# Negated score maxima: from four-row scratch and small transfers to rows written in place

## The reference

```python
xn = layernorm(layernorm(x), gamma, beta)
q = (xn @ w_q).reshape(B, 256, 16, 64);  k, v = split(context @ w_kv)      # 16 heads of 64
attn = softmax(einsum('bqhd,bkhd->bhqk', q * 64 ** -0.5, k))
x = x + tanh(g_xattn) * (einsum('bhqk,bkhd->bqhd', attn, v) @ w_out + b_out) * tanh(gate)
# then a mixture of 8 experts: top-1 routing, 160 slots each, relu(t @ w1[e]) @ w2[e]
x = x + tanh(g_ffn) * experts(layernorm(x))
```

## Time and profile before

| | |
|---|---|
| device time, median of 3 runs | 587.85 us (586.03 to 588.67) |
| the profiled execution's own time | 586.77 us |
| its span in the trace | 585.0 us |
| PE busy | 506.5 us, 87% |
| DVE busy | 436.3 us, 75% |
| ACT busy | 360.5 us, 62% |
| POOL busy | 338.2 us, 58% |
| DMA traffic | 91.22 MB, 156 GB/s on average |
| mean granted TensorE clock | 0.961 of full speed |

### The profile page before, as it was taken

How to read it: one execution, slowest core, us unless ns; L and a number is a source line. 1 busy time by engine, 2 the same in 40 slices (tenths; PEclk the granted TensorE clock), 3 DMA queues, 4 the chain that set the end, 5 groups by cost and what they waited for, 6 DMA issues and landing times.

```text
span 585.0 us, 16296 instructions
## 1 busy us (share of the span) xinstructions
PE 506.5 (87%) x5644; PEld 447.7 (77%) x5644; DVE 436.3 (75%) x814; ACT 360.5 (62%) x671; POOL 338.2 (58%) x207
## 2 busy tenths in 40 slices
PE   4657988799989998999899998999899989985294
PEld 3446877698879887888789887988788879775194
DVE  4577977579886889878987988698869897876112
ACT  3445767467765776667675776577667765762041
POOL 4553568637584657646664666466647565665115
PEclk9877999899999999999999999999999999999588
DMA  7886778847785778757775777677757766750201
GB/s 197 192 220 176 188 190 193 212 99 176 167 203 135 171 162 195 164 129 177 167 177 129 174 166 182 140 176 166 172 130 174 166 154 154 167 149 15 91 4 41
DMA packets 48686, 91.22 MB, mean 156 GB/s; under 512 B 6515, under 2 KB 21539, under 8 KB 48656
## 3 DMA queue, kind: packets, MB, share of 16 engines
q1 hardware_dynamic: 47280, 87.53, 64.9%
q0 software_dynamic: 1376, 3.30, 1.6%
HBM read 10.83 MB, written 5.14 MB: 27 GB/s over the span
## 4 chain that ended last, share of the span: by engine, by line
PE 41%; SPq 27%; DMA 11%; issue 8%; DVE 6%; ACT 4%; POOL 1%; DVEq 0%; POOLq 0%; ACTq 0%
SPq L416 10%; DMA ST<-MROW 8%; SPq L418 7%; PE psS L1107 6%; SPq L428 5%; PE psS L1108 5%; PE psX L1187 4%; PE psM L1083 4%; PE psO L1128 3%; PE psO L1130 2%; PE psO L1129 2%; DVE MX L805 2%; ACT P L662 2%; SPq L433 2%; PE psKQ L1021 2%
## 5 line engine op out<-in xcount | busy, mean ns | idle before, releaser
L558 POOL TENSOR_TENSOR PARTS<-P,PARTS 128x1024 f16<-128x1024 f32 x128 | 274.6, 2146 | 182.9 <-ACT PARTS L706 114.3
L662 ACT ACTIVATE P<-psS 128x512 f32<-128x512 f32 x256 | 146.3, 599 | 62.6 <-PE psS L1108 57.3
L805 DVE TENSOR_REDUCE MX<-psM 128x2 f32<-128x1024 f32 x128 | 155.8, 1217 | 15.9 <-PE psM L1083 15.1
L1107 PE MATMUL psS<-ST 128*128 128x256 f32 x512 | 144.9, 310 | 25.3 <-DMA ST<-MROW 20.4
L1107 PEld LDWEIGHTS psS<-ST 128*128 128x128 f32 x512 | 97.7, 191 | 44.0 <-issue 27.1
L1108 PE MATMUL psS<-ST 128*128 128x256 f32 x512 | 131.0, 283 | 0.0
L1128 PE MATMUL psO<-VH,PARTS 128*128 128x65 f16 x1024 | 108.1, 196 | 2.2 <-POOL PARTS L558 1.6
L1129 PE MATMUL psO<-VL,PARTS 128*128 128x64 f16 x1024 | 106.9, 193 | 0.0
L1130 PE MATMUL psO<-VH,PARTS 128*128 128x65 f16 x1024 | 106.6, 194 | 0.0
L622 ACT ACTIVATE HL<-psKQ 128x768 fp32r<-128x768 f32 x62 | 50.4, 812 | 79.7 <-PE psKQ L1023 76.4
L1108 PEld LDWEIGHTS psS<-ST 128*128 128x128 f32 x512 | 98.4, 192 | 1.0
(11 more groups left out here) (168 smaller groups left out, 818.8 us busy)
## 6 DMA issues: line engine op xcount, KB each, us to landing
ST<-HL SPq DMA_DIRECT2D x128, 384.0 KB, 5.4
ST<-HL SPq DMA_DIRECT2D x128, 192.0 KB, 4.9
ctx_raw<-in_ctx_dram SPq DMA_DIRECT2D x8, 256.0 KB, 4.7
ST<-MROW SPq DMA_DIRECT2D x128, 1.0 KB
w1s<-in_L_ffn_w_dram SPq DMA_DIRECT2D x8, 256.0 KB, 4.7
w2s<-in_L_ffn_w_dram SPq DMA_DIRECT2D x8, 256.0 KB, 3.2
experts_table<-O POOLq DMA_DIRECT2D x2, 645.0 KB, 8.0
PARTS<-experts_table SPq DMA_DIRECT2D x2, 516.0 KB, 4.2
```

The costliest lines, as they stand in the source:

```text
L558: pool.tensor_tensor(PLO[:, par, h, :], P32[:, h, :], PHI[:, par, h, :], ALU.subtract).then_inc(plo_done, 1)
L662: act.activation(P32[:, h, 512 * (c % 2):512 * (c % 2) + 512], psS[c % 2][:], ACT.Exp, scale=SCALE).then_inc(exp_done, 1)
L805: dve.tensor_reduce(MX[:, hp % 2, h, :], psM[:], AX.X, ALU.max, negate=True).then_inc(max_done, 1)
L1107: pe.matmul(dst, ST[:, buf, h, AK + P * kt:AK + P * kt + P], ST[:, buf, h, AQ:STW], start=True, stop=False)
```

## The change

- `MX` grows from 128x(2x2x2) to 128x(2x2x128) and is set to zero once. For each of the two query tiles there is a 128x128 tile, all zero but for two columns: 64 + qt holds the negated maxima of head 0, 96 + qt those of head 1. DVE's reduction writes these columns (a stride of 129 elements between the two it writes).
- `max_transpose` transposes both 128x128 tiles into `psKQ`, columns 768 to 1023. Row 64 (65 for the second query tile) now has head 0's maxima, row 96 (97) head 1's, the others are zero.
- `max_row` copies rows 64 to 97 of 256 columns to `ST` itself, once for each of the two heads of the buffer by a broadcast operand: 34 rows of 2x256. It waits for the buffer's old scores to be done.
- The key side gets 0.0 in place of 1.0 in the rows of the other head, so that each head sees its own maximum only. `LIFT` becomes 1.875 in the 30 rows 98 to 127.
- `MROW`, `max_rows` and their semaphores are gone; `scores` waits for ACT's copy.

Core of the diff:

```diff
-    LIFT = 0.875
+    LIFT = 1.875
+    ROW_H, ROW_END = (64, 96), 98
...
-        MX = sb("MX", [P, 2, 2, QT], F32)
-        MROW = sb("MROW", [2 * QT, 2, P], F32R)
+        MX = sb("MX", [P, 2, QT, P], F32)
...
-            def max_rows(b, hp):
-                j = b * PAIRS + hp
-                buf, par = hp % BUFS, hp % 2
-                sp.wait_ge(mrow_done, j + 1)
-                for h in range(2):
-                    dst = ST[64:65, buf, h, BQ:BK].bitcast(F32)
-                    sp.dma_start(dst, MROW[QT * h:QT * h + QT, par, :].bitcast(F32)).then_inc(mrow_in[par], 16)
...
+            pool.memset(MX[:], 0.0).then_inc(mx_zero, 1)
             pool.wait_ge(pool_consts, 1)
-            pool.memset(ST[:].bitcast(F32)[64:128, :, :, BQ:BK], LIFT).then_inc(stack_consts, 1)
+            pool.wait_ge(mx_zero, 1)
+            pool.memset(ST[:].bitcast(F32)[96:128, :, :, BQ:BK], LIFT).then_inc(stack_consts, 1)
...
+            for h in range(2):
+                r = ROW_H[1 - h]
+                pool.memset(ST[:].bitcast(F32)[r:r + QT, :, h, BK:AK], 0.0).then_inc(stack_consts, 1)
...
                 act.wait_ge(mt_psum, j + 1)
-                if not (is_first(b) and hp < 2):
-                    act.wait_ge(mrow_in[hp % 2], mrow_value(*back(b, hp, 2)))
-                act.activation(MROW[:, hp % 2, :], psKQ[0:2 * QT, KQ:KQ + P], ACT.Copy).then_inc(mrow_done, 1)
+                if not (is_first(b) and hp < BUFS):
+                    act.wait_ge(score_psum, 4 * j - 4 * (BUFS - 1))
+                rows = slice(ROW_H[0], ROW_END)
+                act.activation(ST[rows, hp % BUFS, :, BQ:BK],
+                               psKQ[rows, KQ:KQ + SQ].unsqueeze(1).to_broadcast([ROW_END - ROW_H[0], 2, SQ]),
+                               ACT.Copy).then_inc(mrow_done, 1)
...
-                dve.tensor_reduce(MX[:, hp % 2, h, :], psM[:], AX.X, ALU.max, negate=True).then_inc(max_done, 1)
+                r = ROW_H[h]
+                maxima = bass.AP(MX[:].tensor, MX[:, hp % 2, 0, r:r + 1].offset, [MX[:].ap[0], [P + 1, QT]])
+                dve.tensor_reduce(maxima, psM[:], AX.X, ALU.max, negate=True).then_inc(max_done, 1)
...
-                maxima = MX[:, hp % 2].rearrange("p h q -> p (h q)")
-                pe.transpose(psKQ[0:2 * QT, KQ:KQ + P], maxima, ident[:]).then_inc(mt_psum, 1)
+                for qt in range(QT):
+                    last = pe.transpose(psKQ[:, KQ + P * qt:KQ + P * qt + P], MX[:, hp % 2, qt, :], ident[:])
+                last.then_inc(mt_psum, 1)
...
-                    pe.wait_ge(mrow_in[hp % 2], mrow_value(b, hp))
+                    pe.wait_ge(mrow_done, b * PAIRS + hp + 1)
```

More of the change, by code:

```diff
@@ L202, in gated_block @@
         stack_consts = sem("stack_consts")
+        mx_zero = sem("mx_zero")
+        ones_set = sem("ones_set")
         stats_done = sem("stats_done")
@@ L226, in gated_block @@
         mrow_done = sem("mrow_done")
-        mrow_in = [sem(f"mrow_in{i}") for i in range(2)]
         score_psum = sem("score_psum")
@@ L299, in stack_value @@
             return b * (64 * PAIRS // BUFS) + 64 * (hp // BUFS + 1)
-        def mrow_value(b, hp):
-            return b * (32 * PAIRS // 2) + 32 * (hp // 2 + 1)
         def v_group(b, hp):
@@ L433, in x1_store @@
                 sp.dma_start(out_b[b], x_now).then_inc(x1_out, 16)
-            for hp in range(AHEAD - 1):
+            for hp in range(AHEAD):
                 stacks(0, hp)
-            sp.wait_ge(stack_consts, 1)
-            max_rows(0, 0)
-            stacks(0, AHEAD - 1)
             sp.dma_start(bo[:], b_out.rearrange("(o n) -> o n", o=1).to_broadcast([P, D])).then_inc(bo_in, 16)
@@ L449, in batch @@
                         sp.dma_start(ctx_raw[:], ctx_t[b + 1]).then_inc(ctx_in, 16)
-                    if not (is_last(b) and hp + 1 >= PAIRS):
-                        max_rows(*next_pair(b, hp, 1))
                     if not (is_last(b) and hp + AHEAD >= PAIRS):
@@ L493, in _ @@
             pool.wait_ge(rstd_done, 1)
-            pool.memset(ST[:].bitcast(F32)[64:128, :, :, BK:AK], 1.0).then_inc(stack_consts, 1)
-            pool.wait_ge(stack_consts, 2)
+            pool.memset(ST[:].bitcast(F32)[64:128, :, :, BK:AK], 1.0).then_inc(ones_set, 1)
+            pool.wait_ge(ones_set, 1)
+            for h in range(2):
+                r = ROW_H[1 - h]
+                pool.memset(ST[:].bitcast(F32)[r:r + QT, :, h, BK:AK], 0.0).then_inc(stack_consts, 1)
+            pool.wait_ge(stack_consts, 3)
             pool.memset(VH[:, :, :, DH:DH + 2], 1.0).then_inc(stack_consts, 1)
@@ L675, in _ @@
                         split_w(part)
+            act.wait_ge(stack_consts, 1)
             max_row(0, 0)
@@ L922, in _ @@
             both_variances(*XCHUNKS[1])
+            dve.wait_ge(mx_zero, 1)
             row_max(0, 0, 0)
@@ L1221, in _ @@
             v_project(0, 0, 2)
-            pe.wait_ge(stack_consts, 3)
+            pe.wait_ge(stack_consts, 4)
             max_scores(0, 0, 0)
```

## The result

The changed kernel takes 569.56 us (median of 4 runs, 566.65 to 570.67) beside 588.25 us for the kernel before on the same chip: a ratio of 0.9682, 95% interval 0.9636 to 0.9728, or 18.7 us less. Its profiled execution, the fastest of the four, has a span of 564.9 us, so 20.1 less than the 585.0 of before, where 15 were forecast.

A forecast was written before the change was run, and what follows sets the result against it. PE, busy 58.15 of a loop batch's 61.62 us, was taken as close to the bound. Gains of 26.9 less 10.5, 0.1 and 1.3 gave 15 us off the 585.0 span, 570.0, and a median of 572; range 562 to 582.

The forecast's parts named there:

- gains by the waits that go: First score matmul of a slot: all 26 waits for the maxima's transfers go, with restart and clock losses; 26.9 us.
- two padded transposes: PE, `max_transpose`: two full-width transposes replace a narrow one, 0.19 us more in each of 55 slots; 10.5 us lost.
- DVE's waits that grow: PE's waits for DVE: some grow where PE comes earlier, as DVE has little rest; 1.3 us lost.
- I count nothing: SP and DMA: 128 issues go, stacks keep their start and lose only delays; taken as 0 us.
- the 0.26 added to each of 26 waits: Score matmul's waits: shown idle time understates each by 0.26 us, through modelled end and restart; 6.8 us in all.
- every slot but nine: Transposes' cost hidden only at slot 7 of seven batches and two slots at the start; 55 slots pay 0.19 us.
- Rival C: `max_transpose` and `q_project`, every slot: transposes not overlapping cost more than is saved; 4 us slower, 592; chance 0.06.
- spare time of 0.38: ACT's wider copy before `q_project` on PE: it ends at 307.04, `q_project` is due at 307.42, 0.38 us to spare.
- Rival D: `scores`: the wait only changes its name, to ACT's copy; no change in time; chance 0.04 with other ways to none.
- rival A: Loop batches: DVE's chain takes over, only start, batches 0 and 1 and end gain; 8 us, 579; chance 0.20.
- rival B: Whole kernel: low clock after 46.62 goes, transposes cheaper, DVE's waits don't grow, its two places won; 564; chance 0.15.
- PE waits for DVE above 15 us in total: PE's waits for DVE: a total over 15 us was named as a sign that the forecast is wrong.

The follow-up runs named there:

- e12: e6 with two transposes of the padded 128 columns in place of the narrow one, copy and small transfers as before; 589.93 us.
- e5: The changed kernel with DVE's `slot_now` moved behind the maximum's first half and VL of slot 0 of the next batch; 563.48 us.
- e1: The changed kernel with two useless small transfers a slot back on SP, and the score matmul waiting for them; 595.20 us.
- e6: The kernel before with `slot_now` moved behind the maximum's first half and VL of slot 0 of the next batch; 584.83 us.
- e11: e5 with two transfers of 1 KB a slot issued by SP again, which nobody on PE waits for; 567.56 us.
- e2: The changed kernel with the two useless small transfers a slot on SP, but no score matmul waiting for them; 572.66 us.
- e10: e5 with each of the two padded transposes done twice, into the same place; 570.74 us.
- e13: e5 with ACT's copy of 34x512 done twice in each slot, the first into a tile that nobody reads; 582.86 us.
- e8: e5 with the padded tiles cut from 128 to the 98 columns that are needed; 561.64 us.
- e14: The changed kernel with `slot_now` in its old place, computed by two one-column instructions with one tensor input each; 563.22 us.
- e3: The kernel before with the maxima's two small transfers issued by ACT behind its copy in place of SP; 600.27 us.

## Why the prediction was right, point by point

**The time.** 572 was forecast and 569.6 measured, in the likeliest case. Its last step has a slip: 571.8 for a profiled run, and a median 1.1 above that, give 572.9 and not 572. The parts were not all right either; what they measured:

| term | forecast | measured |
|---|---|---|
| gains by the waits that go | 26.9 | 25.3 (e12 to e5); 26.8 by span, 24.5 by ratio (e1) |
| two padded transposes | -10.5 | -4.8 (e6 to e12) |
| DVE's waits that grow | -1.3 | -1.9 (5.8 of meetings after, 3.9 before) |
| sum | 15 | 18.6 |

The measured column leads from the kernel before by e6, e12 and e5 to the changed kernel, so it must add up to the change's 18.7 but for rounding; only its single values are evidence, and each is uncertain by 3 us or more. That 572 came so near is in part luck: the transposes cost 5.7 us less than forecast, and the gains, in which several pieces were counted too low, came out a little smaller than forecast.

**The gains** were read rightly, as a whole: that shown idle time understates a wait, and that the long waits at the start and the end count most. I held that DVE's reduction at 45.85 would not move and that slot 0 would gain nothing; both came earlier (1.75 and 1.1 us). I left out the low clock behind 46.62; it went, which is worth up to (1 - 0.53) x 6.00 = 2.8 us of full-rate work. And "I count nothing" for SP was too low by some 2.6 us if e11 is right, which its interval leaves open. All these go one way, so that something else among the 26.9 must have been counted too high by as much or more, perhaps the 0.26 added to each of 26 waits; no run separates it. The waits themselves are worth 22.5 to 24.0 us (e1 to e2).

**The transposes** are the term that was mis-sized. The local spacing was nearly right, 0.14 for 0.19. The first full-width load is hidden behind `values` but for some 0.03: from the first transpose to the second are 0.14, and not the 0.20 that I had taken from the score matmul in that place, beside 0.11 in a run of such matmuls. The larger error is the next step, that every slot but nine pays it in full. With 64 x 0.14 = 9.0 on PE only 4.8 came out (e12), and 0.11 of e10's 0.22 (its median to L1026 is 0.71, e5's 0.49). Half of what is added at this place is made up elsewhere. Where, no run here separates. Rival C (592) falls with this: nothing like a bare latency of 0.27 is paid.

**ACT** is right: 594 ns for 581, hidden, and the wait behind it shrank from 76.4 to 53.9 us. The spare time of 0.38 was 0.23 to 0.30 (e13). I had worked it out from one slot, in which ACT was not late. With the upper bound of 0.84 for the copy, 0.26 more, it would have been about used up. Rival D is rejected: no score matmul waits for the copy.

**POOL** is right: MX took 0.52 (0.5 said), the two new fills 3.69 together (3.6 said), and `w_lo` starts at 18.62 for 18.56.

```profile
1.53 0.52 POOL L472 MEMSET MX<- 128x512 f32 x1
...
8.47 3.69 POOL L485 MEMSET ST<- 2x2048 f32 x2
18.62 1.27 POOL L491 TENSOR_TENSOR w_lo<-PARTS,w_hi 128x512 fp32r<-128x512 f32 x1 [6.18 <-ACT w_hi L581]
```

**DVE** had the wrong reason. Its size stays open: 1.9 us by the ratios is uncertain by more than 4, and by the batches the meetings cost 3.3 us in five after (60.23 for 59.57) and 3.1 before (61.37 for 60.75), nearly the same. I took the 1.7 us at each batch head for DVE being the slower engine there (rival A's argument too). It was one addition of 0.16 us that took 2 us, at five heads before and four after. With the addition out of the way a loop batch takes 59.3 to 59.6 us although DVE does the same work, so DVE's 10 us of rest were real. One wait for DVE did grow by the change, of the kind that the prediction had in mind: the load of L1019 waits 2.0 us in 6 places for `cT_lo`, and the kernel before has 0.2 in 1. Rival A (579) is rejected: the five loop batches gained 5.7 us. Of rival B the clock behind slot 1, the smaller transposes and DVE's places came true, but its 564 was not reached.

**The signs named beforehand.** Right: no wait of the score matmul on a transfer, the copy's time, the full clock at 112 to 116, and most of the gain ahead of 175 us (12.65 of 20.1). The sign "PE waits for DVE above 15 us in total" was badly put: PE's waits for DVE add up to 30.0 us before and 30.6 after, and only the transpose's, 11.7, is what was meant. Not so: the transposes' spacings (0.14 and 0.03 for 0.20 and 0.11); behind the loop only 1.7 us were won, the loop gave more than thought, and its batches of 59.1 us lie below the 60.3 to 61.4 named, beside others of 61.0.

**A better version.** Moving `slot_now` or giving it one input takes 6 to 7 us more off. The lowest median is e8's 561.64 (ratio 0.9546, 0.9495 to 0.9598), 1.8 below e5's on the same chip; e14, on another chip, cannot be told from it. e14 with 98 columns was not run.

## What to carry to other kernels

A wait for a small transfer can cost more than its shown idle time (here 20.4 us shown, 22.5 to 24.0 lost). To judge it, put a useless transfer in the same place, once with the wait (e1) and once without (e2); the difference is the wait. Time added to a nearly full matrix engine is not all paid: take the local spacing as the upper end and measure how much comes out. When batches of a loop alternate between two lengths, compare instruction by instruction the heads of a long and a short one before any theory on engines: here one line had two durations, and one operand form cured it.

## What the runs showed of the hardware

- A 128x2 addition on VectorE with two SBUF tensor inputs takes 0.16 us alone, and up to 2.15 when a GpSimd instruction of 2.14 that reads SBUF started 10 ns ahead; if it starts 1.62 us into that one, it takes 0.54. With a scalar of each row in place of the second tensor, one column at a time, it takes 0.20 to 0.22 in all 16 cases (e14), and a 128x512 one with one input in PSUM takes 0.68 beside such a GpSimd instruction (L791 in e5) and 0.69 on average.
- Issuing two small transfers takes 2.28 us on ACT (e3), and ACT's next instruction waits 2.48 us for it.
- Transposes of 128 float32 columns in a row on a full engine add 0.11 us each to the local spacing (0.49 to 0.71 for two more), and about half of that to the time of the kernel (0.87 us a batch of eight slots, e10).
- Loads of 98 columns instead of 128 made no difference that can be seen in the loop (59.54 and 59.57 us a batch).
- Copying 34x512 on ACT takes as long (594 ns) as 128x512 (581): the elements of a row decide here, not the number of rows. On GpSimd filling 2x2048 takes 1.85 us and 64x2048 took 1.80.
